# A two-layer feature-interaction network in fp32: small matmuls over zeros run on the matmul engine before the first weights are ready

## The reference

```python
def _cin_forward(x, Ws):          # x: (512, 39, 64), W0: (39, 39, 128), W1: (39, 128, 128)
    x0 = x
    h = x
    outs = []
    for W in Ws:
        h = jnp.einsum('bid,bjd,ijh->bhd', x0, h, W)
        outs.append(h)
    out = jnp.concatenate(outs, axis=1)
    return out.sum(axis=-1)       # (512, 256)
```

## Time and profile before

| | |
|---|---|
| median of 3 runs | 356.93 us (356.2 to 357.13) |
| the profiled execution, its time | 357.09 us |
| its span, first to last instruction | 355.3 us |
| PE busy | 341.1 us, 96% of the span, 5,688 MATMULs |
| PE weight loads busy | 321.8 us, 91%, 5,688 LDWEIGHTS |
| DVE busy | 152.8 us, 43% |
| ACT busy | 114.7 us, 32% |
| POOL busy | 10.2 us, 3% |
| instruction fetches (a DMA queue of its own) | 44 packets, 0.72 MB |

### The profile page before, as it was taken

How to read it: one execution, slowest core, us unless ns; L and a number is a source line. 1 busy time by engine, 2 the same in 40 slices (tenths; PEclk the granted TensorE clock), 3 DMA queues, 4 the chain that set the end, 5 groups by cost and what they waited for, 6 DMA issues and landing times.

```text
span 355.3 us, 11893 instructions
## 1 busy us (share of the span) xinstructions
PE 341.1 (96%) x5688; PEld 321.8 (91%) x5688; DVE 152.8 (43%) x182; ACT 114.7 (32%) x210; POOL 10.2 (3%) x14
## 2 busy tenths in 40 slices
PE   0899999999998999999999999999999999999997
PEld 0566699999997999999999999999999999999996
DVE  3104559910039535808172680808177171903000
ACT  1266643333364052233205222421422141232300
POOL 9100000000000000000000000000000000000000
PEclk9999999999999999999999999999999999999999
DMA  8940334000022000820000063000006000000000
GB/s 307 383 96 2 136 161 148 2 1 2 2 57 96 2 4 4 199 100 4 17 2 4 2 160 141 2 18 2 4 3 145 9 2 17 4 2 4 4 0 15
DMA packets 4352, 20.06 MB, mean 56 GB/s; under 512 B 592, under 2 KB 1104, under 8 KB 3920
## 3 DMA queue, kind: packets, MB, share of 16 engines
q1 hardware_dynamic: 3728, 18.79, 16.3%
q10 hardware_dynamic: 576, 0.52, 0.4%
HBM read 18.78 MB, written 0.52 MB: 54 GB/s over the span
## 4 chain that ended last, share of the span: by engine, by line
PE 96%; DMA 1%; DVE 1%; issue 1%; SPq 0%; ACT 0%
PE out_ps L508 36%; PE stage L474 35%; PE stage L435 8%; PE stage L455 7%; PE stage L457 7%; PE stage L438 2%; DMA arena<-in_w_rows 1%; DVE arena L270 1%; DVE arena L272 0%; SPq L238 0%; ACT arena L399 0%
## 5 line engine op out<-in xcount | busy, mean ns | idle before, releaser
L508 PE MATMUL out_ps<-arena 114*128 114x128 f32 (+2 forms) x968 | 128.7, 294 | 0.0
L474 PE MATMUL stage<-arena 128*60 128x80 f32 (+4 forms) x4096 | 126.0, 227 | 1.6 <-issue 1.6
L474 PEld LDWEIGHTS stage<-arena 128*50 128x50 f32 (+2 forms) x4096 | 123.6, 128 | 3.7 <-issue 1.9
L508 PEld LDWEIGHTS out_ps<-arena 114*128 114x128 f32 (+1 forms) x968 | 121.7, 192 | 5.2
L408 ACT COPY arena<-stage 114x480 f32<-114x480 f32 (+4 forms) x136 | 72.5, 540 | 136.6 <-PE stage L474 136.6
L334 DVE TENSOR_TENSOR arena<-arena 128x3200 f32<-128x3200 f32 x16 | 55.8, 3487 | 59.6 <-PE stage L474 59.5
L435 PE MATMUL stage<-arena 128*128 128x380 f32 (+1 forms) x78 | 35.5, 539 | 10.0 <-DVE arena L272 10.0
L455 PE MATMUL stage<-arena 128*114 128x128 f32 x234 | 44.7, 273 | 0.0
L457 PE MATMUL stage<-arena 128*114 128x128 f32 x234 | 44.7, 273 | 0.0
L457 PEld LDWEIGHTS stage<-arena 128*114 128x114 f32 x234 | 33.6, 178 | 0.0
L455 PEld LDWEIGHTS stage<-arena 128*114 128x114 f32 x234 | 33.6, 178 | 0.0
(11 more groups left out here) (21 smaller groups left out, 35.1 us busy)
## 6 DMA issues: line engine op xcount, KB each, us to landing
arena<-in_x_dense SPq DMA_DIRECT2D x8, 640.0 KB, 6.4
arena<-in_x_single SPq DMA_DIRECT2D x16, 320.0 KB, 4.9
arena<-in_c_first SPq DMA_DIRECT2D x1, 2560.0 KB, 8.8
arena<-in_w SPq DMA_DIRECT2D x2, 640.0 KB, 6.8
arena<-in_c_second SPq DMA_DIRECT2D x1, 1280.0 KB, 5.2
arena<-in_w SPq DMA_DIRECT2D x1, 1216.0 KB, 9.5
arena<-in_w_square SPq DMA_DIRECT2D x1, 800.0 KB, 4.1
arena<-in_c_one SPq DMA_DIRECT2D x2, 256.0 KB, 9.8
```

What stands on the lines that cost most here:

```text
L474: done = nc.tensor.matmul(bank[PART * part:PART * part + r1 - r0, 0:count * 2 * some] .rearrange("p (i b) -> p b i", b=2 * some)[:, 2 * (t ...
L508: done = nc.tensor.matmul(to, sums, w, start=tile == 0 and s == 0, stop=last, skip_group_check=True)
```

## The change

POOL zeroes `single0` first of all. PE waits for that alone, and then runs a loop of 4 rounds. A round has 8 steps, and in a step each of eight tiles of the array (2 halves of the rows by 4 strips of 32 columns) gets 115 moving columns of zeros, with 32 columns of zeros as weights. In two of the strips the 115 columns are one matmul, in the other two they are two (49 and 66, or 67 and 48). That is 12 matmuls in a step, 96 in a round, 384 in all, and so 768 MATMULs and 768 LDWEIGHTS of PE. One half of the rows writes to `out_ps`, the other to the ring's last bank; both are overwritten by later matmuls that begin a new sum. The round is a loop of the instruction stream (`Fori`): its 96 matmuls, which are 384 instructions of PE, stand once in the program, and a branch goes back to the first three times.

Since the loop reads `single0`, SP now also waits for the first `filled` (PE's first bank of real work) before it loads x into it.

```diff
--- before.py
+++ after.py
@@ -152,6 +152,8 @@
         out_copied = sem("out_copied")
         out_stored = sem("out_stored")
 
+        WARM_ROUNDS, WARM_PAIRS, WARM_WIDTH = 4, 8, 115
+        WARM_PARTS = [[(0, 115)], [(0, 115)], [(0, 49), (49, 115)], [(0, 67), (67, 115)]]
         W1_PIECES = [(0, 10), (10, 20), (20, FIELDS)]
         PASSES = BATCHES * TILES
         UNITS = 2 * PASSES
@@ -199,6 +201,7 @@
 
         @block.gpsimd
         def _(pool):
+            nc.gpsimd.memset(view(single0, (1, 2 * PAIRS * SLOTS)), 0.0).then_inc(single_zeroed, 1)
             ident = view(ident0, (1, HID))
             nc.gpsimd.memset(ident, 0.0).then_inc(ident_zeroed, 1)
             pool.wait_ge(ident_zeroed, 1)
@@ -214,7 +217,6 @@
                 nc.gpsimd.memset(view(z_own0[h], (1, HALF * W_SPAN)), 0.0).then_inc(z_zeroed, 1)
             zero_between(0)
             nc.gpsimd.memset(view(y0[1] + (HALF - 1) * Y_WIDTH[1], (1, Y_WIDTH[1])), 0.0).then_inc(z_zeroed, 1)
-            nc.gpsimd.memset(view(single0, (1, 2 * PAIRS * SLOTS)), 0.0).then_inc(single_zeroed, 1)
 
             pool.wait_ge(z_ready, 1)
             zero_between(1)
@@ -245,7 +247,9 @@
             sp.wait_ge(w0_ready, 2)
             for hf in range(2):
                 load_dense(0, hf)
+
             sp.wait_ge(single_zeroed, 1)
+            sp.wait_ge(filled, 1)
             for hf in range(2):
                 load_single(0, hf)
             sp.wait_ge(z_ready, 1)
@@ -420,6 +424,19 @@
                 if g >= RING:
                     pe.wait_ge(emptied, g - RING + 1)
                 return banks[g % RING]
+
+
+            pe.wait_ge(single_zeroed, 1)
+            with pe.Fori(0, WARM_ROUNDS):
+                for r in range(WARM_PAIRS):
+                    for strip, parts in enumerate(WARM_PARTS):
+                        for c0, c1 in parts:
+                            for s in range(2):
+                                rows = (s * P // 2, (s + 1) * P // 2)
+                                nc.tensor.matmul(
+                                    (out_ps, banks[RING - 1])[s][32 * strip:32 * strip + 32, c0:c1],
+                                    view(single0 + 32 * (r + strip), (1, 32), rows=rows),
+                                    view(single0 + r * WARM_WIDTH + c0, (1, c1 - c0), rows=rows), start=True, stop=True)
 
             g = 0
             pe.wait_ge(w0_ready, 2)
```

## The result

The changed kernel takes 359.69 us (median of 4 runs, 359.33 to 360.4) against 356.74 before (356.2 to 357.13): ratio 1.0086, 95% interval 1.0065 to 1.0107. Slower, but by 2.95 us and not by 18.8. The profiled execution took 359.66 us, its span is 357.9 us against 355.3.

The account below looks back on a forecast made before the run. It took PE to bound the kernel: 5.15 + 4 x 3.10 + 3 x 3.73 = 28.75 us for the first real matmul against 9.96, so 357.09 + 18.8 = 375.9 us. The whole range was 358 to 382.

Parts of the forecast that it names:

- Bound by PE: Whole kernel: PE is busy 96% of the span, so moving its first real matmul moves the end as much.
- start at 5.15: Start of the loop: POOL's zeroing of `single0` is done at 5.10 us, and PE starts at about 5.15.
- break-even at 13.0: Start of the real work: begun at full clock at 13.0 us, it ends when it ends now.
- Instruction fetch: Loop's branches back, the term given most weight: each refetches the first block, 3.73 us idle, three times, 11.2 us.
- the quiet 71 us: From 27 to 98.4 us before the change: 1,119 PE instructions, five packets, read as no room for blocks ahead.
- The clock: PE in the loop: idling between bursts keeps it at 1.2 GHz, so the real work still pays 3.05 us.
- slow start: First fields of the real work before the change: run at 1.2 GHz instead of 2.4, costing 3.05 us.
- One step: A step of the loop: 0.39 us slow, 0.20 us fast; nothing charged for instruction issue.
- The first rival: Loop: the body stays in PE's memory, no fetches, loop ends at 14.5 us, total 358.6 us; chance 0.24.
- The two stops: PE's instruction-issue stops at 111.10 and 114.83 us, 1.8 us: shifted block boundaries change them either way, taken as nothing.
- The sign: Whole kernel: slower by more than 0.3% (1.1 us) 0.84, within it 0.10, faster 0.06.

Follow-up runs that it names:

- e4: Changed kernel with its 32 steps written out once, 1,536 instructions and no branch back; 374.07 us (one run).
- e5: Changed kernel with two rounds of sixteen steps, a loop body of 768 instructions; 369.18 us (one run).
- e12: Changed kernel with two rounds of 32 steps, a loop body of 1,536 instructions; 384.56 us (one run).
- e3: Changed kernel with no split matmuls, one of 115 columns per tile and step, 16 instead of 24 MATMULs a step; 358.44 us (one run).
- e8: Changed kernel with two rounds of eight steps and 70 columns instead of 115, the same 24 MATMULs a step; 353.58 us, ratio 0.9918.
- e1: Changed kernel without its loop, POOL's early zeroing and SP's wait kept; 356.41 us against 356.52 before the change, ratio 1.0005.
- e6: Changed kernel with six rounds of five steps, a loop body of 240 instructions; 360.85 us (one run).
- e7: Changed kernel with each of the 32 steps as one whole-array matmul of 115 columns, passed once, 128 instructions; 356.56 us (one run).
- e11: Changed kernel with PE waiting only for 1,024 words zeroed first, and 32 written-out whole-array matmuls of 100 columns, weights of 128, for the loop; 353.62 us.
- e2: Changed kernel with half the loop, two rounds of eight steps; 354.02 us, ratio 0.9945.
- e9: Changed kernel with POOL zeroing 1,024 words first, PE waiting for those alone, and three rounds of eight steps; 353.19 us, ratio 0.9916.
- e13: Changed kernel with PE waiting only for 1,024 words zeroed first, and 32 written-out matmuls of 100 columns, weights of 64, for the loop; 352.82 us.

## Why the prediction was wrong

*Bound by PE, start at 5.15, break-even at 13.0.* Right: the loop began at 5.22, and real work that began at full pace at 16.84, 3.8 us past the break-even, brought the main loop 3.9 us late.

*Instruction fetch: the step that failed.* "PE holds the block it runs and one more" and "that takes the first one's place". The rows showed that blocks are asked for one at a time, when the one before is entered; I concluded from it how many are kept. These are different things. e4 shows the first: 3.5 to 6.0 us for each new block. e5 and e12 refute the second: at least six blocks stayed. The three ways back cost 0.3 us each, not 3.73: 0.9 us instead of 11.2. That only five packets came in the quiet 71 us shows that no more were asked for, not that there was no room. The Trainium skill, Runtime: NRT & Kernel Launch, Instruction fetch mechanics, gives PE 128 KiB of instruction memory; e12 agrees as far as it goes (1,536 instructions are 96 KiB, and no run tried more). Its sentence in the same section on a window of two pages doesn't hold for a way back on this engine: in e12 the branch leads from the seventh block to the first, with no packet.

*The clock.* I had it stay low in the loop, as a consequence of the gaps. That stops of this length can bring it down, e4 shows: in its first, of 3.8 us, it fell. Without gaps it rose 4.7 us after the start. This took the real work's slow start away, 3.0 us.

*One step.* 0.39 us slow was nearly right (3.3 us for eight, 0.41 each). Fast it was 0.28 instead of 0.20: after seeing four instructions begin within 20 ns, a burst, I charged nothing for the split matmuls, and they cost 0.08 us a step (e3 against the changed kernel). How they cost it is open: one instruction in 5.8 ns is not a fixed limit, since e8 had one in 5.4 (384 in 2.08 us). Some 21 fast steps were 0.08 us longer each, 1.7 us, and the slow ones 0.2 in all. The first rival, which is what happened, had the loop end at 14.5: 14.5 + 1.9 + 0.9 for the ways back, less 0.7 for the earlier rise of the clock, is 16.6; measured 16.84. That its 358.6 us lies so near the 359.66 of the profiled execution is in part luck: the loop ended 2.3 us later than it said, and 1.8 us of stops, which it took as nothing, went.

*The two stops* were "between 1.8 us less and as much more, taken as nothing". They went, 1.84 us, in the changed kernel, and were the part of the change that helped beside the clock. What decides most of it is where the blocks begin, so how many instructions stand in front. PE's idling marked "issue" at the small matmuls, as each run's page has it, was 1.6 us before. It was 1.2 to 1.4 where the number in front is nought or near a whole number of blocks: none (e1), 240 (e6), 256 (e3), 768 (e5), 1,536 (e4, e12). It was 0.0 to 0.2 with half a block over: 128 (e7, e11) and 384 (changed kernel, e2, e9); but 0.4 in e13 and 0.7 in e8, with the same numbers in front. How late the real work starts doesn't decide it: e12 starts last and has them, e2 starts early and hasn't. By the rows, a block lasts 3.0 us in a pass of 40 columns and 4.4 in one of 80, so only in the former does PE outrun a fetch of 3.5. Why almost nothing of the stops is left in some runs, and 0.7 us in e8, isn't shown. No run moved the blocks alone, without the warming.

*The sign* was right, but not by the term I gave most weight: with no refetch the loop is still too long, 11.6 us where 8 were to spare.

## What to carry to other kernels

Idle time of PE before the first operands can be used to get its clock up, for 3 us at most here, if the filler ends when the operands come: count it at the slow pace, and start it as early as its own input allows (e9 and e13). When a program's start moves by some hundred instructions, look whether a stop for instruction fetch later in it came or went before crediting the edit. From how something is prefetched, don't conclude how much is kept; a count of the instruction queue's packets tells it.

## What the runs showed of the hardware

- PE's program came in blocks of 256 instructions, asked for one at a time. A new block took 3.5 to 3.7 us from the entry of the one before, 5.9 to 6.0 with the DMA engines full (e4). Blocks already brought stayed: a body of 1,536 instructions was repeated without a fetch (e12).
- A branch back cost 0.3 us, for bodies of 240 (e6) and 384 instructions (changed kernel), both over a block's boundary.
- The clock rose 2.5 to 6.1 us after PE's first matmul (e8: 2.5, e9: 2.6, e2: 2.8, e1: 3.2, changed kernel: 4.7, before: 6.1), with tiles as with the whole array (e7, e11). So the slow start cost 1.6 us in one execution and 3.05 in another.
- With zeros in eight tiles, a pair of weight load and MATMUL began every 11.7 ns in the changed kernel's fast steps and every 10.8 in e8's second round. Weights of 128 columns held a matmul of 100 columns to 0.22 us (e11); with weights of 64 it took 0.17 (e13).
